# A fused scan and mixture-of-experts layer on one core: one-hot inversion in one run, D*u in the fold's matmuls, gathers 4 tiles ahead

## What is computed

```python
h = exp(delta_t * A) * h + (delta_t * u_t) * B_t      # 256 channels x 16 states
y_t = sum over the states of h * C_t, plus D * u_t    # D: one factor for each channel
```

## Time and profile before

| | us |
|---|---|
| median of 3 runs (909.78 to 914.67) | 912.57 |
| the profiled execution's own time | 911.35 |
| its span, first to last instruction | 909.3 |
| busy in the span: VectorE / TensorE / GpSimd / ScalarE | 711.9 / 645.2 / 617.1 / 417.6 |

### The profile page before, as it was taken

How to read it: one execution, slowest core, us unless ns; L and a number is a source line. 1 busy time by engine, 2 the same in 40 slices (tenths; PEclk the granted TensorE clock), 3 DMA queues, 4 the chain that set the end, 5 groups by cost and what they waited for, 6 DMA issues and landing times. The chain is left out here.

```text
span 909.3 us, 15177 instructions
## 1 busy us (share of the span) xinstructions
PE 645.2 (71%) x4254; PEld 410.5 (45%) x4255; DVE 711.9 (78%) x889; ACT 417.6 (46%) x862; POOL 617.1 (68%) x388
## 2 busy tenths in 40 slices
PE   3630667615878787797787879779788878878871
PEld 2410355402555554454454545445545544545541
DVE  5889763631999999889989799899989988998210
ACT  1310333513556664564565456456546645644320
POOL 3727860001687888887887887788888878878642
PEclk9755568856999999998999799899989988979996
DMA  8644764992455365456446436635654654453332
GB/s 219 238 141 123 257 212 145 286 359 81 103 130 123 82 150 123 81 130 136 87 104 146 102 81 142 129 81 118 136 117 97 130 119 97 109 122 75 47 41 23
DMA packets 76699, 118.73 MB, mean 131 GB/s; under 512 B 22184, under 2 KB 56704, under 8 KB 74368
## 3 DMA queue, kind: packets, MB, share of 16 engines
q1 hardware_dynamic: 54656, 90.95, 36.5%
q0 software_dynamic: 19824, 27.16, 16.9%
q10 hardware_dynamic: 2192, 0.28, 0.4%
HBM read 83.00 MB, written 35.27 MB: 130 GB/s over the span
## 5 line engine op out<-in xcount | busy, mean ns | idle before, releaser
L546 POOL TENSOR_TENSOR ring<-ring,bc 128x1024 f32<-128x1024 f32 x128 | 316.5, 2487 | 43.3 <-DVE state L1073 41.0
L1069 DVE TENSOR_TENSOR_SCAN ring<-ring,state,pb 128x512 f32<-128x512 f32 x256 | 313.8, 1267 | 4.6
L1288 PE MATMUL py<-w2x,pool 128*128 x568 | 166.6, 446 | 5.6 <-ACT late L683 3.3
L665 ACT ACTIVATE ring<-late,aneg 128x512 f32<-128x512 f32 x256 | 163.8, 713 | 0.3
L1060 DVE TENSOR_TENSOR pb<-fb,bc 128x1024 f32<-128x1024 f32 x128 | 157.3, 1229 | 3.0
L519 POOL DMA_INDIRECT out_dram<-pool,meta x71 | 112.4, 1583 | 66.4 <-DMA out_dram<-late,idb 50.6
L1275 PE MATMUL fa<-w,pool 128*128 x284 | 143.9, 631 | 6.4 <-issue 5.3
L503 POOL DMA_INDIRECT pool<-xn_d,meta x71 | 71.5, 1008 | 110.1 <-DMA meta<-tab 81.7
L1288 PEld LDWEIGHTS py<-w2x,pool 128*128 128x128 f32 x568 | 121.6, 225 | 27.7 <-issue 8.7
L1275 PE MATMUL fb<-w,pool 128*128 x284 | 133.7, 593 | 0.0
L1261 PE MATMUL pt<-ident,pool 128*128 128x128 f32 x138 | 32.5, 322 | 141.5 <-DMA pool<-xn_d,meta 138.9
(11 more groups left out here) (214 smaller groups left out, 725.2 us busy)
## 6 DMA issues: line engine op xcount, KB each, us to landing
late<-dd_d SPq DMA_DIRECT2D x256, 128.0 KB
bc<-bc_d SPq DMA_DIRECT2D x72, 256.0 KB
w<-in_L_ffn_w_dram SPq DMA_DIRECT2D x16, 512.0 KB, 10.5
ring<-in_L_attn_x_dram SPq DMA_DIRECT2D x8, 512.0 KB, 4.4
xn_d<-w2x SPq DMA_DIRECT2D x8, 512.0 KB, 4.4
out_dram<-ring SPq DMA_DIRECT2D x8, 512.0 KB
dd_d<-pool SPq DMA_DIRECT2D x8, 512.0 KB, 3.6
w2x<-in_L_ffn_w_dram SPq DMA_DIRECT2D x8, 512.0 KB, 5.7
```

The source lines that it names most:

```text
L546: ins = po.tensor_tensor(r, r, c_rows, ALU.mult)
L665: ins = ac.activation(ring[:, g % RING, n, :], dd[:, g % 2, 0, :], ACT.Exp, scale=aneg[:, NH * g + n:NH * g + n + 1])
L1069: ve.tensor_tensor_scan(r, r, pb[:, CH * m:CH * m + CH], state[:, NH * g + n:NH * g + n + 1], ALU.mult, ALU.add).then_inc(S["scan_done"], 1)
L1288: ins = pe.matmul(py[:, 0:D], ht[:, P * k:P * k + P], w2[:, bass.ds(e * (HC * D) + D * k, D)], start=(k == 0), stop=(k == HC - 1))
```

## The change

- The stored start of `out` is plain `x`, from the loaded tiles, ahead of the weights; `start_sums` is gone. `D * u` is added in `fold_states`: the transposed sorted rows `ut` go to a new DRAM array `u_d` (`store_u`), each unit's 32 channels come back (`load_u`, in SyncE's turn), and four more matmuls with a diagonal matrix `skip` add them.
- The one-hots are made and inverted ahead of the chunks, with three buffers each. VectorE does all of `oh_b` but the probabilities, which ScalarE multiplies in (`weigh`). `tab` is ready after chunk 0, and no weights wait for it but `w3`.
- Gathers run 4 tiles ahead into 4 buffers. For this SyncE's turn waits for one more transposed tile, and loads the `meta` of tile `j + 4`.
- On GpSimd the scan add stands before the multiplies.

```diff
 SyncE, before the loop
+            acc_v = out[0:TOK, :].rearrange("(q j p) d -> q p j d", p=P, j=TPC)
+            for q in range(NCH):
+                sp.wait_ge(x_sem[q % 2], 16 * (q // 2 + 1))
+                sp.dma_start(acc_v[q], xin[:, TPC * q:TPC * q + TPC, :]).then_inc(S["acc_put"], 16)
+            for e in range(E):
                 load_up(e, w1, w1_in)
...
+            def load_u(c, g):
+
+                if not (isinstance(c, int) and c == 0 and g < 2):
+                    sp.wait_ge(S["sum_done"], unit_index(c, g) - 1)
+                    apart(sp)
+                sp.dma_start(ug[:, g % 2, :], u_d[bass.ds(unit_index(c, g) * DG, DG), :]).then_inc(ug_in[g % 2], 16)
...
                 store_dd(c)
                 if c == 0:
                     for h in range(2):
                         sp.wait_ge(S[f"xs_put{h}"], 16 * NT // BATCH)
                     sp.wait_ge(S["xn_put"], 16 * (NCH + 1))
+                    sp.wait_ge(S["inv_step"], NGRP)
+                    sp.wait_ge(S["tab_ready"], 1)
+                    for j in range(5):
+                        if j >= 2:
+                            sp.wait_ge(meta_in[j % 2], 16 * (j // 2))
+                        load_meta(j, j, j % 2)
+                load_down(c)
+                load_up(c, w3, w3_in)
 SyncE, turn(c); load_dd(c, s) stays at its head
                     j = SPI * c + 1 + s
-                    sp.wait_ge(S["xtr_done"], j + 1)
+                    sp.wait_ge(S["xtr_done"], j + 2)
...
-                    load_meta(j + 3, (s + 4) % SPI, s % 2)
+                    load_meta(j + 4, (s + 5) % SPI, (s + 1) % 2)
+                    if not (isinstance(c, int) and s < 2):
+                        load_u(c, s)
                     if 3 <= s < 3 + P // DG:
                         load_bc((c + 1) % NCH, (c + 1) % 2, [s - 3])
 GpSimd, turn(c)
-                    gather(SPI * c + 3 + s, (s + 3) % SPI, (s + 1) % 2)
+                    gather(SPI * c + 4 + s, (s + 4) % SPI)
+                    if s in SCAN_STEPS and not isinstance(c, int):
+                        add_scan(expert_turn(c, s) - 1, c - 1, SCAN_STEPS.index(s))
                     po.wait_ge(S["h_ready"], unit_index(c, s) + 1)
...
                         ins = po.tensor_tensor(r, r, c_rows, ALU.mult)
-                        if half == 0 and s in SCAN_STEPS and not isinstance(c, int):
-                            add_scan(expert_turn(c, s) - 1, c - 1, SCAN_STEPS.index(s))
 ScalarE, new
+            def weigh(g):
+
+                ac.wait_ge(S["oh_b_done"], g + 1)
+                for t in range(GRP):
+                    at = GRP * g + t
+                    ins = ac.activation(oh_b[g % HOT][:, t, 1, :], oh_b[g % HOT][:, t, 1, :], ACT.Copy,
+                                        scale=prf[:, at // NT, at % NT:at % NT + 1])
+                ins.then_inc(S["oh_p_done"], 1)
 TensorE, fold_states
+                pe.wait_ge(ug_in[g % 2], 16 * (c * (G // 2) + g // 2 + 1))
...
+                for q in range(TPC):
+                    ins = pe.matmul(pz[DG * q:DG * q + DG, 256:384], skip[:, DG * g:DG * g + DG], ug[:, g % 2, P * q:P * q + P],
+                                    start=False, stop=True, tile_position=(0, DG * q))
                 ins.then_inc(S["sum_done"], 1)
 TensorE, before the loop
+            for g in range(NGRP - 2):
+                invert(g)
             turn_rows(0)
+            invert(NGRP - 2)
             for c in range(NCH):
                 project(c)
-                if 0 < c < NCH - 1:
+                if c == 0:
+                    invert(NGRP - 1)
+                if c < NCH - 1:
                     turn_rows(c + 1)
                 project_delta(c)
```

More of the change, by code:

```diff
@@ L72, in program @@
         w3 = sb("w3", [P, E * KC * H])
[L73 to L78, removed]
+        oh_b = [w3[:, h * GRP * 2 * FTP:(h + 1) * GRP * 2 * FTP].rearrange("p (t a j) -> p t a j", t=GRP, a=2)
+                for h in range(HOT)]
+        oh_a = [w3[:, 3456 + h * GRP * P:3456 + (h + 1) * GRP * P].rearrange("p (t j) -> p t j", t=GRP) for h in range(HOT)]
+        spare = w3[:, 6528:7040]
         iota128 = spare[:, 0:P]
@@ L236, in program @@
         dd_in = [S["dd_in0"], S["dd_in1"]]
-        xr_in = [S["xr_in0"], S["xr_in1"]]
+        xr_in = [S[f"xr_in{k}"] for k in range(4)]
+        ug_in = [S["ug_in0"], S["ug_in1"]]
         meta_in = [S["meta_in0"], S["meta_in1"]]
@@ L304, in load_sorted, with store_u @@
                 sp.dma_start(prep[c % 2]["xsr"], xs_v[c]).then_inc(S[f"xs_in{c % 2}"], 16)
[L307 to L312, removed]
+            def store_u(c):
+                sp.wait_ge(S["pr_ut"], KC * (c + 1))
+                sp.dma_start(u_d[D * c:D * c + D, :].rearrange("(k p) t -> p k t", p=P), ut[c % 3]).then_inc(S[f"u_put{c % 3}"], 16)
             def store_dd(c):
@@ L385, in _ @@
                     load_dd(0, 1)
[L387 to L393, removed]
             for n in range(KC * 2):
@@ L398, in _ @@
                 sp.wait_ge(S[f"bc_put{n}"], 32 * NCH // 2)
+            for n in range(3):
+                sp.wait_ge(S[f"u_put{n}"], 16 * ((NCH - 1 - n) // 3 + 1))
+            load_u(0, 0)
+            load_u(0, 1)
             def turn(c):
@@ L480, in _, with gather @@
                 scatter(xs_d, pos_a, t, S[f"xs_put{t // (NT // BATCH)}"])
[L481 to L497, removed]
+            def gather(j, slot):
+                fixed = isinstance(j, int)
+                po.wait_ge(meta_in[slot % 2], 16 * (j // 2 + 1) if fixed else 8 * j + (16 if slot % 2 == 0 else 8))
+                if not fixed:
                     apart(po)
-                if not isinstance(j, int) or j >= 2:
-                    po.wait_ge(S["xtr_done"], j - 1)
-                if not isinstance(j, int):
+                if not fixed or j >= 4:
+                    po.wait_ge(S["xtr_done"], j - 3)
+                if not fixed:
                     apart(po)
-                po.indirect_dma_start(xr[:, parity, :], None, xn_d[:, :],
-                                      bass.IndirectOffsetOnAxis(ap=meta.bitcast(U32)[:, slot, 0:1], axis=0)).then_inc(xr_in[parity], 16)
+                po.indirect_dma_start(xr[slot % 4], None, xn_d[:, :],
+                                      bass.IndirectOffsetOnAxis(ap=meta.bitcast(U32)[:, slot, 0:1], axis=0)).then_inc(xr_in[slot % 4], 16)
             po.wait_ge(S["xn_put"], 16 * (NCH + 1))
@@ L508, in _ @@
             po.wait_ge(S["pr_ids"], NCH - 1)
-            for j in range(3):
-                gather(j, j, j % 2)
+            gather(0, 0)
+            gather(1, 1)
+            for h in range(KC):
+                po.wait_ge(S[f"dd_put0{h}"], 16 * NCH // 2)
+            gather(2, 2)
+            gather(3, 3)
             def add_expert(turn, j, slot, parity):
@@ L572, in _ @@
                                     for k in range(KC)),
-                                  (dsb, ds_in.rearrange("(o d) -> o d", o=1).to_broadcast([P, D])),
+                                  *((dcol[:, g:g + 1], ds_in[DG * g:DG * g + DG].rearrange("(p o) -> p o", o=1)) for g in range(G)),
                                   *((aneg[DG * q:DG * q + DG, :].rearrange("p (g n) -> p g n", g=G),
@@ L859, in _ @@
             ve.engine_nop().then_inc(S["sqrt_v"], 1)
[L861 to L871 removed]
             ve.wait_ge(S["const2_in"], 16 * CONST2_LOADS)
[L874 to L875 removed]
+            ve.wait_ge(S["pool_const"], 1)
+            ve.tensor_tensor(skip[:, :].rearrange("p (g d) -> p g d", g=G),
+                             ident[0:DG, 0:DG].rearrange("p (o d) -> p o d", o=1).to_broadcast([DG, G, DG]),
+                             dcol.rearrange("p (g o) -> p g o", o=1).to_broadcast([DG, G, DG]), ALU.mult).then_inc(S["skip_ready"], 1)
             ve.wait_ge(S["ln_rows1"], NT // 2)
@@ L1076, in _ @@
             for g in range(NGRP):
-                tile_hot(g)
-            for g in range(2):
-                row_hot(g)
+                one_hots(g)
+                if g in (4, 6):
+                    cluster_rows(g // 2 - 2)
+            last = NB - 1
+            link(ve.tensor_tensor(ge[:, :, 0:last], jt.rearrange("p (j o) -> p j o", o=1).to_broadcast([1, FTP, last]),
+                                  ct[0:1, 0:last].rearrange("p (o k) -> p o k", o=1).to_broadcast([1, FTP, last]), ALU.is_ge))
+            link(ve.tensor_reduce(etf, ge[:, :, 0:last], AX, ALU.add))
+            link(ve.tensor_copy(etab[:, :], etf))
             take_ids(0)
```

131 lines of the change are left out of this document (53 added, 78 removed).

## The result

The changed kernel takes **1149.22 us** (median of 4 runs, 1142.34 to 1152.25) against 912.47 (4 runs, 909.78 to 914.67): a ratio of 1.259, with a 95% interval of 1.252 to 1.266. The forecast said 1086, in a range of 1000 to 1130. The direction and the mechanism are those of the forecast; the size is not, 237 us where it had 175. The profiled execution took 1151.28 us, its span 1149.5.

A forecast was written before the change was run, and what follows sets the result against it. The loop was taken to be bound by a ring through SyncE's delta loads, once around each turn. From the profiled 911.35 us, minus 16 in the preparation, plus 191 in the loop: 1086 us, range 1000 to 1130.

The forecast's parts named there:

- The ring: Loop: one round trip per turn, transposes to SyncE's delta loads to ScalarE's exps to next transposes; plus 191 us.
- rival 1, the short trip: Loop: ring closes, but loads land in 3.9 us in all turns and the clock holds; 990 us, chance 0.12.
- the landing in plain turns: Loop, turns without B and C loads: delta loads land 4.1 us after the first issue.
- rival 2: Loop: delta loads are early after all and GpSimd sets the loop; 885 us, chance 0.09.
- the mean turn, 12.8 us: Loop: mean of plain turns at 11.15 us and turns with B and C loads at 14.45.
- the part from the exps to the transposes: Loop: exps' start to next transposes, 4.6 us before clock allowance; 4.9 plain and 5.2 with B and C.
- from the transposes to the loads: Loop: SyncE's way to the delta loads, 2.15 us plain and 3.35 with B and C, load of u included.
- run beside `evac_ht` and cost nothing here: TensorE's fold in the loop: the four added matmuls are covered and add no time.
- The uncovered 0.3 of the forecast: TensorE's fold in the loop: the four added matmuls' cost if not covered, some 0.3 us.
- The clock: TensorE in the loop: lower level adds up to 1.2 us; half taken in long turns, a quarter in others.
- The scan add "costs nothing": GpSimd in the loop: scan turn of 11 to 12 us is covered by turns of 11 to 14.
- The preparation: Before the loop: 23.5 MB at 317 GB/s set it, first turn at 208 for 223.9; minus 16 us.

The follow-up runs named there:

- run 2: Kernel before with only SyncE's wait changed, to the transposes of one more tile (j+2 for j+1): 1104.5 us.
- run 1: Changed kernel with SyncE issuing the delta loads of unit s+1 at the head of turn s, before the long wait: 894.27 us, ratio 0.979.
- runs 9 and 10: Changed kernel without the D*u path, 1081.75 us; and changed kernel with the load of u issued behind the delta loads, 1108.51 us.
- run 9: Changed kernel without the D*u path (no stores and loads of u, no skip matmuls): 1081.75 us.
- run 3: Changed kernel with the delta loads directly behind SyncE's wait, ahead of meta, u, B and C: 921.26 us.
- run 4: Changed kernel with two spare matmuls in each turn of TensorE, ahead of its wait for ye_done: 1130.87 us.
- run 5: GpSimd's scan add put back between the halves of the multiplies, on top of run 1: 882.83 us, ratio 0.970.
- run 6: run 1 without the D*u path (stores and loads of u, skip matmuls): 881.18 us, ratio 0.968.
- run 7: run 1 with meta loads spread over chunks 1 to 5 and w3 a chunk later, so SyncE isn't held in chunk 0: 887.52 us, ratio 0.973.

## Why the forecast was right in kind and wrong in size

- **The ring: right.** Which wait closes it (run 2), which loads are in it (run 1), who stands behind ScalarE (the waits after) and the two lengths of turns are as forecast. Against rival 1, the short trip: the landing in plain turns is 4.83, where it needed 3.9. Against rival 2: 62 waits of the exps. 191 us had been forecast for the wait and the DMA of `u` in it; the wait alone brings 194 of loop, and the DMA 47 more.
- **The step that failed is the working of the mean turn, 12.8 us, in three of its terms** (measured 13.75 over the 61 turns, 61 us in the loop). Of the 61 us the part from the exps to the transposes has some 21, the one from the transposes to the loads 20, and the landing 14: 22 more in the plain turns, 9 less in those with B and C. First, "run beside `evac_ht` and cost nothing here": the four added matmuls of the fold were costed as covered. With TensorE in the ring they are on the path: at the lower clock (granted 0.50 from 633.5 to 634.2) they took 0.65 us behind a fold that ends after `evac_ht`, and runs 9 and 10 put them at 0.2 to 0.5 a turn, 13 us in the loop by the profiles and some 21 by the medians. Without them, in run 9, this part is 5.11 and 4.83, as forecast. The uncovered 0.3 of the forecast should have been in the sum. Second, the landing in plain turns, taken as 4.1 from gathers that land singly: 4.83 with the load of `u` in front, 4.52 without. A load of `delta` takes 3.2 us in plain turns, not the gathers' 2.8, unless it is issued ahead of the others (run 3). Third, from the transposes to the loads, 2.54 for 2.15 and 3.60 for 3.35. The load of `u` was nearly right there (0.65 for 0.55); but without it the path is 1.84, where the earlier trace rows gave 1.60, and the transposes at its start run at the lower clock (0.69 for 0.44 us).
- **The clock: right in the end, and partly by luck.** Half and a quarter of 1.2 us were taken, and no row gave these shares. Run 9's last part is 5.11 and 4.83, the forecast 5.2 and 4.9. The low clock itself is dear on TensorE (816 us busy), and much cheaper for the kernel as far as run 4 took it back, since ScalarE's copies run beside the fold.
- **That run 9 meets the forecast, with 1081.75 and a loop of 809.5, is partly chance:** it lacks the 0.55 us for the load of `u` that the forecast has in each turn, and its other terms are about as much longer than forecast.
- **The scan add "costs nothing": right in the closed ring, wrong with the ring open.** The forecast's scan turn of 11 to 12 us was right (11.05). It is hidden by turns of 12.6 and 14.8, and costs 9 to 13 when they are gone (run 5). Even so the loop of run 1, 608.2 us, is what rival 2 had (some 10 less than 617.8). That the kernel came to 894 and not to its 885 lies outside the loop: it begins 5 us later than 208, and 70.8 us follow it for 67.6.
- **The preparation: 10.2 us won for 16; the bytes were counted short, and that is most of it.** SyncE was free at 123.05, as forecast. TensorE begins the loop's tiles at 203.60, behind the landing of all of `w1` and `w3`, and the first turn follows 10.1 us later (11 forecast). The stretches from 123, columns of the earlier trace rows:

```profile
123.00:130.00 7.00, 0.00 (x0) 0.00 (x0) 5.71 (x10) 1.63 (x4) 0.00 (x0) 0.71 0.81 208
130.00:190.00 60.00, 31.82 (x120) 15.73 (x120) 24.38 (x40) 22.51 (x42) 1.96 (x2) 0.50 1.05 331
190.00:196.00 6.00, 0.00 (x0) 0.00 (x0) 0.00 (x0) 0.00 (x0) 0.28 (x1) 0.50 1.04 405
196.00:203.60 7.60, 0.00 (x0) 0.03 (x1) 0.00 (x0) 0.00 (x0) 1.61 (x2) 0.50 0.53 196
```

  Rate by length and added up, these are 25.2 MB in 80.6 us, 313 GB/s in the mean. The rate was forecast at 317; the bytes at 23.5 MB, and with these it would have been 197. The queues are full from 130 on, and the last 7.6 us run half empty while the last weights land. At 317 GB/s 25.2 MB would have ended at 202.6. Fewer bytes won 5.8 us in run 6; the 2 us of run 7, which starts the queues earlier, are within what executions differ by.
- **The end** is nearly as forecast, 66.0 for 67.6.

## What to carry to other kernels

In an in-order queue, a wait that is moved later moves everything behind it: before a wait's number is changed, list each later issue of that queue and the consumer that needs it, and count the turns between them. If that count falls to nothing, the loop has become a ring, and then an instruction in it counts, however well it was covered before (the load of `u` alone: 41 us in the ring by the medians; all of D*u with the ring open: 5 us of loop, run 6). The remedy is to issue the prefetch ahead of the wait (run 1), or at least directly behind it (run 3).

## What the runs showed that was not expected

- Raising TensorE's granted clock from 0.763 to 0.839 in the mean won only 18 us of 1149 (run 4), though the fold takes 1.08 us at the one level and 1.94 at the other.
- The same load of 128 KB lands in a median of 2.8 us when it is issued first (run 3) and in 3.8 behind `meta` and, in half of the turns, B and C (run 2), though the DMA engines are busy for only 39% of the changed kernel's loop. One DMA of `u` more in front goes with 0.3 us more of landing in plain turns (4.83 us against 4.57 and 4.52), and with none in turns with B and C.
- The exps take 2.56 us for four, and `turn_y` began 2.97 us after them at either clock. With the ring closed this chain of one engine's copies is in every turn's path, in a kernel whose VectorE is idle for a third of the loop.
